# Order of the three products inside a unit: each block's wh*xh, wh*xl and wl*xh one after the other

## What is computed

```python
x1, x2 = (x[:, :F], x[:, F:])
h1 = leaky_relu(layer_norm(x1 @ W1.T))
h2 = leaky_relu(layer_norm(x2 @ W1.T))
h1 = leaky_relu(layer_norm(h1 @ W2.T))
h2 = leaky_relu(layer_norm(h2 @ W2.T))
h = jnp.concatenate([h1, h2], axis=-1)
h = leaky_relu(layer_norm(h @ W3.T))
return h @ W4.T
```

## Time and profile before

| | us |
|---|---|
| median of 3 runs | 250.47 (249.77 to 251.3) |
| span of the profiled execution, first to last instruction | 247.5 |
| TensorE busy / VectorE busy / ScalarE busy | 240.1 / 185.4 / 169.7 |
| the three lines of the first product, 320 matmuls each | L487 88.7, L492 126.1, L494 125.7 |

### The profile page before, as it was taken

One profiled execution on the slowest core, in us unless ns is written; L12 is line 12 of the kernel. 1 busy time (PEld: TensorE's weight loads), 2 busy tenths in 40 slices (PEclk: granted clock), 3 DMA queues, 4 the chain that ended last, 5 costly groups with the idle time before them and its releaser, 6 DMA issues.

```text
span 247.5 us, 4093 instructions
## 1 busy us (share of the span) xinstructions
PE 240.1 (97%) x1096; PEld 196.2 (79%) x1096; DVE 185.4 (75%) x369; ACT 169.7 (69%) x320; POOL 8.9 (4%) x19
## 2 busy tenths in 40 slices
PE   7899999999999999999999999999999999999992
PEld 2588888888888888888888888888888888888882
DVE  3799999989565898777667589777756589877333
ACT  4798999876767567667568577667677756767150
POOL 2000000000000300000000110000000020000002
PEclk9999999999999999999999999999999999999996
DMA  6999899975455358666624358766625545761000
GB/s 193 394 316 319 311 301 357 347 222 169 141 171 171 125 171 252 214 187 216 188 91 155 106 170 252 246 183 216 192 91 169 169 160 167 249 197 75 0 0 1
DMA packets 15270, 47.35 MB, mean 191 GB/s; under 512 B 2080, under 2 KB 2464, under 8 KB 15264
## 3 DMA queue, kind: packets, MB, share of 16 engines
q1 hardware_dynamic: 15264, 47.28, 58.3%
HBM read 47.27 MB, written 0.00 MB: 191 GB/s over the span
## 4 chain that ended last, share of the span: by engine, by line
PE 93%; DMA 2%; DVE 1%; SPq 1%; POOL 1%; issue 1%; POOLq 0%; DVEq 0%
PE acc L492 29%; PE acc L494 29%; PE acc L487 29%; PE h_ps L521 3%; DMA w_raw<-w 2%; PE h_bank L537 1%; PE var_bank L544 1%; PE h_bank L553 1%; DVE x_lo L347 0%; POOL inv L213 0%; DVE w_lo L322 0%; POOL inv L215 0%; SPq L173 0%; SPq L171 0%; SPq L180 0%
## 5 line engine op out<-in xcount | busy, mean ns | idle before, releaser
L492 PE MATMUL acc<-x_lo,w_hi 128*128 128x512 f32 x320 | 126.1, 394 | 1.2 <-DVE x_lo L347 0.8
L494 PE MATMUL acc<-x_hi,w_lo 128*128 128x512 f32 x320 | 125.7, 393 | 0.0
L244 ACT CAST x_hi<-x_raw 128x1024 fp32r<-128x1024 f32 x76 | 79.9, 1051 | 45.1 <-PE acc L494 36.6
L347 DVE TENSOR_TENSOR x_lo<-x_raw,x_hi 128x1024 fp32r<-128x1024 f32 x79 | 96.1, 1216 | 0.0
L322 DVE SCALAR_TENSOR_TENSOR w_lo<-w_raw,w_mean,w_hi 128x256 fp32r<-128x256 f32 x160 | 70.2, 480 | 30.5 <-ACT w_hi L221 29.5
L487 PE MATMUL acc<-x_hi,w_hi 128*128 128x512 f32 x320 | 88.7, 395 | 0.1
L221 ACT ACTIVATE w_hi<-w_raw,w_mean 128x256 fp32r (+1 forms) x160 | 72.5, 501 | 3.0 <-DVE w_mean L424 1.9
L492 PEld LDWEIGHTS acc<-x_lo,w_hi 128*128 128x128 f32 x320 | 60.3, 189 | 16.1 <-DVE x_lo L347 1.2
L487 PEld LDWEIGHTS acc<-x_hi,w_hi 128*128 128x128 f32 x320 | 59.7, 189 | 13.8 <-ACT x_hi L287 0.6
L494 PEld LDWEIGHTS acc<-x_hi,w_lo 128*128 128x128 f32 x320 | 60.4, 189 | 12.8
L352 DVE SCALAR_TENSOR_TENSOR a_fm<-h_fm 128x256 f32<-128x256 f32 (+2 forms) x20 | 7.8, 421 | 11.4 <-ACT h_fm L259 11.1
(11 more groups left out here) (48 smaller groups left out, 47.9 us busy)
## 6 DMA issues: line engine op xcount, KB each, us to landing
x_raw<-x SPq DMA_DIRECT2D x79, 512.0 KB, 4.2
w_raw<-w SPq DMA_DIRECT2D x19, 256.0 KB, 3.5
x_raw<-x SPq DMA_DIRECT2D x2, 256.0 KB, 3.2
w_raw<-w SPq DMA_DIRECT2D x2, 128.0 KB, 2.4
w_raw<-w SPq DMA_DIRECT2D x1, 64.0 KB, 2.9
w_sb<-w SPq DMA_DIRECT2D x2, 8.0 KB, 3.2
out<-y SPq DMA_DIRECT2D x1, 4.0 KB, 1.4
```

Source lines behind the costliest of these rows:

```text
L244: act.copy(x_hi[:, s, :], x_raw[:, s, :])
L347: dve.tensor_tensor(x_lo[:, s, :], x_raw[:, s, :], x_hi[:, s, :].bitcast(F32), ALU.subtract).then_inc(lo_ready, 1)
L492: pe.matmul(acc[:, g % 2, m, :], wh[:, c, m, :], xl[:, c, :], start=False, stop=False, skip_group_check=True)
L494: ins = pe.matmul(acc[:, g % 2, m, :], wl[:, c, m, :], xh[:, c, :], start=False, stop=True, skip_group_check=True)
```

## The change

In `multiply` the wait for lo stands directly behind the wait for hi, ahead of all the matmuls, and the two loops over chunks and blocks become one: for each chunk and block the three products follow each other.

```diff
                 xh = x_hi[:, s, :].rearrange("p (c n) -> p c n", c=UC)
                 xl = x_lo[:, s, :].rearrange("p (c n) -> p c n", c=UC)
                 pe.wait_ge(*hi)
+                pe.wait_ge(*lo)
                 for c in chunks:
                     for m in blocks:
                         pe.matmul(acc[:, g % 2, m, :], wh[:, c, m, :], xh[:, c, :],
                                   start=(start and c == 0), stop=False, skip_group_check=True)
-                pe.wait_ge(*lo)
-                for c in chunks:
-                    for m in blocks:
                         pe.matmul(acc[:, g % 2, m, :], wh[:, c, m, :], xl[:, c, :],
                                   start=False, stop=False, skip_group_check=True)
                         ins = pe.matmul(acc[:, g % 2, m, :], wl[:, c, m, :], xh[:, c, :],
```

## The result

The changed kernel takes 251.37 us in the median of 20 runs (250.9 to 255.19), the kernel before 250.05 us in the median of 20 runs beside it (249.5 to 251.39). The ratio is 1.0064, 95% interval 1.0043 to 1.0085. (The ratios leave out an execution that is more than 1.5% above the fastest of its kernel, here the one of 255.19 us; the medians count every execution.) The forecast was 251.4 us. The change makes the kernel slower by 0.4 to 0.8%, just about at the bound of what can be told from no change.

A forecast was written before the change was run, and what follows sets the result against it. The prediction took TensorE's matmul stream, busy 97% of the span, as the bound. It summed 0.92 (unit 1) + 0.05 (unit 8) + 0 = 0.97 us onto 250.47, giving 251.4 us, range 250.2 to 252.9.

The forecast's parts named there:

- 2.97 us "around the span": Time outside the profiled 247.5 us span, up to the 250.47 us median of three runs; added unchanged to the forecast span.
- Cost of the moved wait in unit 1: Start-up: all 12 matmuls of unit 1 run behind its x_lo instead of 8, a loss of 0.92 us.
- (a): Instruction count: none added or removed, 12 matmuls and 12 weight loads to a unit, two waits, one signal.
- Unit 0 hidden: Start-up: unit 0 ends at 10.05 or 11.33 us, before unit 1's x_lo at 11.77, so its loss costs 0.
- The time of the clock's rise: Start-up, unit 0: TensorE goes from the 1.2 to the 2.4 GHz level at about 7.4 us.
- Units 2 to 4 covered by the loss itself: Behind unit 1: the 0.92 us already lost covers these units' waits for x_lo, so it is lost only once.
- Order inside a unit free: Every unit: repeated w_hi tile, three products in one bank and changing moving operand leave the 0.2289 us spacing; cost 0.
- third rival: Every unit: a second load of the same w_hi tile makes the following matmul cheaper, 4.9 us, giving 246.5; chance 0.05.
- Unit 8: Three later groups: the weight load comes slightly late behind x_lo, 0 to 0.3 us, taken as 0.05 in all.
- second rival: Unit 8 of three groups: VectorE's serial stretch is longer, each 0.1 us costing 0.3; 251.9 us at 0.2 more; chance 0.09.
- Late clock: Unit 1: clock still low, 0.198 us more for each matmul; 252.2 us taken, 253.8 for all 12; chance 0.16.

The follow-up runs named there:

- e1: Kernel before with only the wait for lo moved to the head of a unit, old matmul order: 251.61 us against 250.18, ratio 1.0053.
- e3: Kernel before with new order and wait at the head only in units 0 and 1 of the first group: 251.35 us against 250.18, ratio 1.0036.
- e6: Changed kernel with 2 warm-up matmuls instead of 8: 251.21 us against 250.04 for the kernel before, ratio 1.0066.
- e2: Changed kernel with units 0 and 1 of the first group kept in the old order: 251.34 us against 250.18 for the kernel before, ratio 1.0043.
- e8: Kernel before with 12 warm-up matmuls instead of 8: 250.15 us against 250.04, ratio 1.0006.
- e5: Changed kernel with 12 warm-up matmuls instead of 8: 251.44 us against 250.04 for the kernel before, ratio 1.0065.
- e9: Changed kernel with the whole first group kept in the old order: 250.42 us against 249.84 for the kernel before, ratio 1.0028.
- e12: Kernel before with three waits: hi*hi, then w_lo*x_hi behind w_lo's wait, then w_hi*x_lo behind x_lo's: 249.10 us against 249.84, ratio 0.9971.
- e7: Kernel before with 2 warm-up matmuls instead of 8: 250.06 us against 250.04, ratio 1.0003.
- e11: Kernel before with one extra VectorE instruction of about 0.42 us ahead of unit 8 in three groups: 249.82 us against 249.84, ratio 1.0003.
- e4: The changed kernel again, unaltered, beside the kernel before: 251.47 us against 250.18, ratio 1.0039.

## Why the prediction was right, and where it was off

The mechanism is the forecast's: four hi*hi of unit 1 that used to run before its x_lo came now run behind it, and nothing later pays for them again. The total of 251.4 us, however, hits the measured 251.37 so closely by luck. It was built on the median of three executions, 250.47, while 20 executions of the kernel before gave 250.05: 0.42 too high. The loss was put at 0.97 where the medians gave 1.32: 0.35 too low. The two cancel. The 2.97 us "around the span" also mix two things: in all later executions, for which both are known, 1.7 to 2.2 us lie outside the span, so about 0.8 to 1.3 us were the distance between the profiled execution and that median.

- **Cost of the moved wait in unit 1 (0.92 us): right, 0.97.** e1 and e3 isolate it: the wait without the order has it, and two units have it alone.
- **"None is added or removed" in (a) was wrong.** The trace counts 4182 instructions instead of 4093, 89 more, and 89 is the number of calls of `multiply` (22 in each of four groups, one more for unit 0's halves); e3, where three calls are changed, has 4096. My reading, that two waits back to back need an instruction for one of them, fits these counts. After a wait the weight load starts 0.11 us behind the end of x_lo (12.07 to 12.18) where it was 0.05 (11.77 to 11.82), and the missing 0.05 us of the distance are that. In a running stream these instructions cost nothing: 47.03 us both times.
- **Unit 0 hidden: right**, in the trace after (three waits of 1.2 to 1.6 us, of which the end sees only the last) and at its extreme in e3 and e6, where unit 0 runs wholly or nearly so at the 1.2 GHz level. The time of the clock's rise, taken from the one trace of before (about 7.4 us), doesn't carry over: in the trace after, the matmuls are 0.23 us apart from 6.49 us on, in e3 0.43 up to 11.54.
- **Units 2 to 4 covered by the loss itself: right**, and e2 shows the other side: with unit 1 in the old order, unit 2 waits.
- **Order inside a unit free: right.** Old and new, 47.03 us from unit 2 to the first mark, so the third rival (a cheaper matmul on a kept tile) is out: its 4.9 us would be 1.0 us in the matmuls of these 17 units. The Trainium skill's 216 ns for a matmul without a weight load's share (TensorE: Matmul & The Clock Gate, Back-to-back issue gap) is reached in neither order: the loads are still made, 320 on each line, and the spacing stays 228.9 ns.
- **Unit 8 (0.05 us): 0.10.** The load comes 0.11 behind x_lo instead of 0.05, and two matmuls of unit 8 start 0.27 us apart instead of 0.23. The second rival didn't come: from mark to mark no trace of the changed kernel has more than that, but for the slower pace of the last section.
- **Late clock (0.16): not the cause of the median**, as unit 1 is at 0.23 us in every profile of the moved wait and the number of warm-up matmuls changes neither median. It is seen in the old order in e8, at 1.57 us, and stays the open candidate for the executions above 254 us, which only kernels with the moved wait in units 0 and 1 have.
- **The size.** The traces give 0.97 + 0.10, about 1.1 us; the medians gave 1.32 and 1.29, and 1.40 and 1.17 in e5 and e6. 1.1 us is a ratio of 1.0044, which lies in all four intervals, near the lower end of three. Yet most kernels whose `multiply` was edited come out above what their trace explains (e2 by 0.6 us, e9 by 0.44, the changed kernel by 0.1 to 0.3), though e12 doesn't, and e7, e8 and e11, whose isn't edited, are at the time of before. What this remainder is stays open. Two candidates: later loads (x_lo of unit 1 ends at 11.42 to 12.42 in the four profiles of unedited code and at 12.07 to 12.89 in the ten others, which overlap), and the slower pace of the last section, which is in five of those ten profiles and in none of the four. Against the second: each of the five profiled executions took 0.5 to 1.3 us more than the median of its kernel, so most executions can't have had it.

## What to carry to other kernels

Where a kernel is bound by an unbroken stream on one engine, a wait moved forward costs the work that used to stand before it, at the place where the wait is the last to end; in this kernel that place was in the start-up, and the mean shares didn't show it. There the loss was paid once, and it then hid the smaller ones in the units right behind it. Look at the longest executions as well as at the median: here the longest grew by more than the median did. The same look shows the gain: put every product that doesn't need the late operand ahead of the wait (e12).

## What the runs showed that was not expected

The stream of matmuls has a second, 2% slower pace that comes and goes, in both orders, at a granted clock of 1.00. Most stretches have 0.2289 us from start to start. In e3, with the old order in these units, a unit of the first group takes 2.80 us instead of 2.746 (0.2333 each):

```profile
29.56 1.10 PE L488 MATMUL acc<-x_hi,w_hi 128*128 128x512 f32 x4
...
32.36 1.10 PE L488 MATMUL acc<-x_hi,w_hi 128*128 128x512 f32 x4
```

It lasted most of the first group in e2, e3 and e12, and from about 148 to 188 us in e4 and e5. By the marks it costs 0.7 to 1.2 us of an execution, as much as the change. So the spans of single profiles (250.4 in e2 and e3, 250.0 in e4) can't be compared without their marks: each of these spans is, to 0.1 us, that of the kernel before plus the later x_lo of unit 1, the longer distance, the cost at unit 8 and this pace (e4: 247.5 + 0.60 + 0.97 + 0.10 + 0.78 = 249.95). What it comes from no run here shows.
